# Set-up of a two-layer perceiver kernel: one load for all weights, X in quarters, row statistics moved into the first cross attention

## What is computed

```python
def _layernorm(x, axis=-1, eps=1e-05):
    m = jnp.mean(x, axis=axis, keepdims=True)
    v = jnp.var(x, axis=axis, keepdims=True)
    return (x - m) / jnp.sqrt(v + eps)

x = x + _L0_xattn_ref(ctx_1024, ctx_1024, _layernorm(x), Wk, Wv, bv, Wq, bq, Wo, bo)   # one head
x = x + _L0_attn_ref(_layernorm(x, axis=-1), ...)
...
```

## Time and profile before

| | |
|---|---|
| median of 3 runs | 1492.5 us (1491.97 to 1501.98) |
| profiled execution | 1493.61 us |
| its span, first to last instruction | 1491.8 us |
| mean granted clock of PE | 0.904 |
| busy: PE, DVE, ACT, POOL | 84%, 67%, 56%, 56% of the span |
| set-up pass | to about 28.8 us |
| first cross attention | about 28.8 to 136 us |

### The profile page before, as it was taken

One profiled execution on the slowest core, in us unless ns is written; L12 is line 12 of the kernel. 1 busy time (PEld: TensorE's weight loads), 2 busy tenths in 40 slices (PEclk: granted clock), 3 DMA queues, 4 the chain that ended last, 5 costly groups with the idle time before them and its releaser, 6 DMA issues. The chain is left out here.

```text
span 1491.8 us, 49249 instructions
## 1 busy us (share of the span) xinstructions
PE 1248.6 (84%) x15586; PEld 1084.6 (73%) x15587; DVE 1006.2 (67%) x3247; ACT 836.9 (56%) x2658; POOL 830.2 (56%) x1700
## 2 busy tenths in 40 slices
PE   3998698887489994999999999999969987369990
PEld 2777688776479993777777777777758877269990
DVE  4774378886446662788888788888759998523334
ACT  1664376664234442777777777777737776135550
POOL 2674035676646663566665666656434577736660
PEclk9997589997589996999999999999979999579995
DMA  7994651221122212322111111111000000122215
GB/s 236 328 361 145 228 157 53 69 69 44 57 64 64 66 54 65 97 65 81 35 38 50 35 53 35 41 47 32 16 16 3 17 29 27 59 56 71 67 59 176
DMA packets 93088, 121.84 MB, mean 82 GB/s; under 512 B 12402, under 2 KB 66931, under 8 KB 92947
## 3 DMA queue, kind: packets, MB, share of 16 engines
q1 hardware_dynamic: 74258, 82.70, 18.2%
q0 software_dynamic: 13312, 34.69, 6.5%
q10 hardware_dynamic: 5376, 2.63, 0.6%
HBM read 89.48 MB, written 30.49 MB: 80 GB/s over the span
## 5 line engine op out<-in xcount | busy, mean ns | idle before, releaser
L1611 ACT ACTIVATE p_prob<-six,p_nm 128x257 f32<-128x257 f32 x512 | 235.9, 474 | 121.5 <-DVE p_nm L1653 120.6
L1653 DVE TENSOR_REDUCE p_nm<-six 128x2 f32<-128x514 f32 x256 | 164.9, 685 | 36.4 <-PE six L1509 34.8
L1863 PE MATMUL bank<-sb_w,m_experts_aT 128*128 x1152 | 155.3, 278 | 2.7 <-ACT m_experts_aT L1892 2.2
L1842 POOL DMA_INDIRECT expert_outputs<-m_experts_y,m_experts_dest x144 | 142.3, 988 | 26.1 <-POOL m_experts_tiny L1841 15.8
L1879 PE MATMUL six<-m_experts_xT,m_experts_w 128*128 128x128 f32 x1152 | 156.0, 279 | 0.0
L791 POOL DMA_INDIRECT expert_inputs<-p_r_x,p_r_slot x128 | 126.2, 986 | 36.5 <-issue 35.6
L1863 PEld LDWEIGHTS bank<-sb_w,m_experts_aT 128*128 128x128 f32 x1152 | 141.3, 193 | 5.8 <-issue 5.6
L1879 PEld LDWEIGHTS six<-m_experts_xT,m_experts_w 128*128 128x128 f32 x1152 | 143.4, 196 | 0.5
L1530 PE MATMUL six<-sb_const,p_prob 128*128 128x128 f32 x1024 | 140.7, 281 | 0.0
L1390 POOL TENSOR_TENSOR p_score<-p_score,p_mx 128x512 f32<-128x512 f32 x64 | 67.1, 1049 | 124.6 <-DVE p_mx L1335 123.1
L1733 POOL TENSOR_TENSOR p_spread<-p_recip,sb_const 128x128 f32<-128x128 f32 x128 | 51.2, 400 | 150.2 <-DVE p_recip L1664 150.1
(11 more groups left out here) (293 smaller groups left out, 3504.5 us busy)
## 6 DMA issues: line engine op xcount, KB each, us to landing
ctxT_ring<-ctxT SPq DMA_DIRECT2D x32, 512.0 KB
ctxN_ring<-ctxN POOLq DMA_DIRECT2D x32, 512.0 KB, 5.5
p_ctxT<-ctxT SPq DMA_DIRECT2D x32, 512.0 KB, 3.6
m_experts_x<-expert_inputs SPq DMA_DIRECT2D x144, 64.5 KB
bd_scores<-p_rows SPq DMA_DIRECT2D x32, 256.0 KB, 2.9
p_bd<-bd_scores SPq DMA_DIRECT2D x32, 256.0 KB
sb_w<-w SPq DMA_DIRECT2D x32, 256.0 KB
p_y<-expert_outputs SPq DMA_DIRECT2D x32, 128.0 KB, 3.3
```

Of the source, the lines that this page charges most:

```text
L1611: last = nc.scalar.activation(prob[:, b, g, :], scores_ps[:, g, 0:CTX], ACT.Exp, bias=nm[:, b % 2, g:g + 1], accum_out=total[:, b % 2, g:g ...
L1653: nc.vector.tensor_reduce(nm[:, b % 2, g:g + 2], scores_ps[:, g:g + 2, 0:CTX], AX.X, ALU.max, negate=True).then_inc(s[most], 1)
L1842: nc.gpsimd.indirect_dma_start(m.ys_dram[:, :], bass.IndirectOffsetOnAxis(ap=dest[:, t.par:t.par + 1], axis=0), y[:, t.par, :], None).then ...
L1863: last = nc.tensor.matmul(ps[6 + t.two][:, 0:D], aT[:, t.two, f * P:(f + 1) * P], m.w2[:, DS(held[p] + f * D, D)], start=(f == 0), stop=(f ...
```

## The change

- The 18 weight matrices become one array of 128 rows of 9216 bytes, and SP loads it by one DMA. It and `const`, `cols`, `rows` are issued ahead of X.
- X is loaded in four quarters of 8 tiles. SP's order is now: quarter 0, context 0, quarter 1, context 1, context 2, quarter 2, context 3, quarter 3.
- In the set-up, DVE makes the statistics of quarter 0 alone, with each aggregation directly behind its own statistics, and POOL the factors and means of quarter 0 on 8 columns.
- In `cross_one_head`, DVE makes the statistics of two tiles in each of the steps 1 to 4, 9 to 12 and 17 to 20 (quarters 1, 2 and 3), between `z` and the maximum. POOL makes a quarter's factors and means in steps 5, 13 and 21, behind the step's context load. From tile 8 on, `z` waits for the factors of its quarter.

```diff
+        self.begun = 0
...
-    def dve_all(self, dve, x_in):
-
+    def dve_quarter(self, dve, q, tiles, bnst):
 
         m, nc = self.m, self.m.nc
-        for n in range(TILES + 1):
-            if n < TILES:
-                if n % HALF == 0:
-                    dve.wait_ge(x_in[n // HALF], 16)
-                if n >= 2:
-                    dve.wait_ge(self.kept, n - 1)
-                nc.vector.bn_stats(self.bnst[:, n % 2, :], m.X[:, n * D:(n + 1) * D]).then_inc(self.stats_done, 1)
-            if n >= 1:
-                dve.wait_ge(self.stats_done, n)
-                nc.vector.bn_aggr(m.mv_all[:, 2 * (n - 1):2 * n], self.bnst[:, (n - 1) % 2, :]).then_inc(self.kept, 1)
-
-    def pool_all(self, pool):
+        for n in tiles:
+            if n % QUARTER == 0:
+                dve.wait_ge(m.x_in[q], 16)
+            if self.begun >= 2:
+                dve.wait_ge(self.kept, self.begun - 1)
+            self.begun += 1
+            nc.vector.bn_stats(bnst[:, n % 2, :], m.X[:, n * D:(n + 1) * D]).then_inc(self.stats_done, 1)
+            dve.wait_ge(self.stats_done, self.begun)
+            nc.vector.bn_aggr(m.mv_all[:, 2 * n:2 * n + 2], bnst[:, n % 2, :]).then_inc(self.kept, 1)
+
+    def pool_quarter(self, pool, q, done):
+
         m, nc = self.m, self.m.nc
-        pool.wait_ge(self.kept, TILES)
-        mv = m.mv_all[:, :].rearrange("p (t k) -> p t k", k=2)
-        f = m.factor[:, :]
-        const = lambda k: m.const[:, k:k + 1].broadcast_to([P, TILES])
-        step = 0
-        for out, a, b in self.forms:
-            for dst, x, y, op in ((f, mv[:, :, 1], a, ALU.mult), (f, f, b, ALU.add), (out[:, :], f, C_POW, ALU.pow)):
-                if step:
-                    pool.wait_ge(self.pool_step, step)
-                nc.gpsimd.tensor_tensor(dst, x, const(y), op).then_inc(self.pool_step, 1)
-                step += 1
-        nc.gpsimd.tensor_tensor(m.MEAN[:, :], mv[:, :, 0], const(C_ONES), ALU.mult).then_inc(self.pool_step, 1)
+        pool.wait_ge(self.kept, QUARTER * (done + 1))
+        tiles = slice(q * QUARTER, (q + 1) * QUARTER)
+        mv = m.mv_all[:, 2 * q * QUARTER:2 * (q + 1) * QUARTER].rearrange("p (t k) -> p t k", k=2)
+        f = m.factor[:, tiles]
+        const = lambda k: m.const[:, k:k + 1].broadcast_to([P, QUARTER])
+        out, a, b = self.forms[0]
+        step = 4 * done
+        for dst, x, y, op in ((f, mv[:, :, 1], a, ALU.mult), (f, f, b, ALU.add), (out[:, tiles], f, C_POW, ALU.pow),
+                              (m.MEAN[:, tiles], mv[:, :, 0], C_ONES, ALU.mult)):
+            if step:
+                pool.wait_ge(self.pool_step, step)
+            nc.gpsimd.tensor_tensor(dst, x, const(y), op).then_inc(self.pool_step, 1)
+            step += 1
...
 RING, EARLY, ENDS = 4, 2, 8
+QUARTER = TILES // 4
...
-            for n in range(2):
-                sp.dma_start(m.X[:, n * 2048:(n + 1) * 2048].rearrange("p (t d) -> p t d", d=D),
-                             m.x_dram[n * 16:(n + 1) * 16].rearrange("t p d -> p t d")).then_inc(x_in[n], 16)
+            def quarter(q):
+                sp.dma_start(m.X[:, q * QUARTER * D:(q + 1) * QUARTER * D].rearrange("p (t d) -> p t d", d=D),
+                             m.x_dram[q * QUARTER:(q + 1) * QUARTER].rearrange("t p d -> p t d")).then_inc(m.x_in[q], 16)
+
+            def context(n):
+                sp.dma_start(m.ctxT[:, n], context_columns(m, n)).then_inc(m.columns_in[n], 16)
+                sp.dma_start(m.ends[:, n], context_ends(m, n)).then_inc(m.columns_in[n], 16)
+
             for dst, src in loads:
                 sp.dma_start(dst, src).then_inc(loaded, 16)
-            for n in range(RING):
-                sp.dma_start(m.ctxT[:, n], context_columns(m, n)).then_inc(m.columns_in[n], 16)
-                sp.dma_start(m.ends[:, n], context_ends(m, n)).then_inc(m.columns_in[n], 16)
+            quarter(0)
+            context(0)
+            quarter(1)
+            context(1)
+            for n in range(2, RING):
+                context(n)
+                quarter(n)
...
-            tail.dve_all(dve, x_in)
+            tail.dve_quarter(dve, 0, range(QUARTER), m.bnst)
...
-            tail.pool_all(pool)
+            tail.pool_quarter(pool, 0, 0)
...
+    m.in_use.extend(columns_in + rows_in + m.x_in)
...
+    given = Tail(m, "p1_given", [sinks(m, "z")])
...
+        given_stats = sb("given_stats", [P, 2, 6])
...
+                    if t.n >= QUARTER:
+                        dve.wait_ge(given.pool_step, 4 * (t.n // QUARTER))
                     normed(m, z[:, t.par, :], t, m.RZ).then_inc(s["z"], 1)
+                q, part = 1 + (n - 1) // QUARTER, (n - 1) % QUARTER
+                if n >= 1 and q < 4 and 2 * part < QUARTER:
+                    first = q * QUARTER + 2 * part
+                    given.dve_quarter(dve, q, range(first, first + 2), given_stats)
...
+                q = 1 + (n - 1) // QUARTER
+                if n % QUARTER == 1 + QUARTER // 2 and q < 4:
+                    given.pool_quarter(pool, q, q - 1)
...
-        m.w = {n: sb("w_" + n, [P, w]) for n, w in WEIGHTS.items()}
+        weights = sb("weights", [P, len(WEIGHTS) * P])
+        m.w = {n: weights[:, k * P:(k + 1) * P] for k, n in enumerate(WEIGHTS)}
         m.setup_loads = [(m.const[:, :], a["const"]), (m.cols[:, :], a["cols"]), (m.rows[:, :], a["rows"])]
-        m.setup_loads += [(m.w[n][:, :], a[n]) for n in WEIGHTS]
+        m.setup_loads += [(weights[:, :], a["weights"])]
...
+        m.x_in = [nc.alloc_semaphore(name=f"x_in_{n}") for n in range(4)]
...
+    a["weights"] = np.concatenate([a.pop(n) for n in WEIGHTS], 1)
```

More of the change, by code:

```diff
@@ L317, in setup_pass @@
     loaded = m.sem("weights_loaded")
-    x_in = [m.sem("x_in_a"), m.sem("x_in_b")]
     folded = m.sem("folded")
@@ L2065 @@
 COLS = ("bq0", "bv0", "bv_a", "bq_a", "bk_a", "u", "v", "gamma", "beta", "norm_w")
-WEIGHTS = {"Wq0": 128, "Wk0": 128, "Wv0": 128, "Wo0T": 128, "Wq_a": 128, "Wk_a": 128, "Wv_a": 128,
-           "Wpos": 128, "Wf": 128, "WqT_x": 128, "WkT_x": 128, "WvT_x": 128, "WoT_x": 128,
-           "w_q": 128, "w_k": 128, "w_v": 128, "w_o": 128, "ctx_last": 128}
+WEIGHTS = ("Wq0", "Wk0", "Wv0", "Wo0T", "Wq_a", "Wk_a", "Wv_a", "Wpos", "Wf", "WqT_x", "WkT_x", "WvT_x", "WoT_x",
+           "w_q", "w_k", "w_v", "w_o", "ctx_last")
 def lay_out(i):
```

1 line of the change is left out of this document (removed).

## The result

The changed kernel took 1487.4 us (median of 20 runs, 1483.1 to 1499.5), the kernel before 1494.1 us in the same comparison (20 runs, 1484.6 to 1502.0). The ratio is 0.9963, with a 95% interval of 0.9946 to 0.9979: by the ratio 5.5 us or 0.37% less (by the two medians 6.7 us), where I had forecast 9.5 us. The time is inside the range of 1478 to 1489 us, and it lies in the band of rival A too (1485.5 to 1490 us). The profiled execution of the changed kernel took 1488.0 us.

What follows compares the result with a forecast made beforehand. Two set-up chains, PE's weights and fold and the DVE/POOL row statistics, were taken as the bound to shorten. 10.2 us gained, less 0.5 and 0.2, is 9.5 us: 1483 us against the median, 1478 to 1489 us.

Steps and rivals of the forecast that it cites:

- rival A: Cross attention gives gain back through DVE's statistics pairs (2.3 to 6.7 us) or tiles blocked by POOL (3.4 us); chance 0.16.
- the slack of the context-row load: Cross attention, POOL's queue: load issued 9.7 us ahead of use, landing in 5.5 us, leaving 4.2 us of slack.
- the bursts: POOL making a quarter's factors and means in cross attention, 2.6 us each: cost 0.1 us per burst, 0.2 in all.
- The tile's own factor: Cross attention, queued behind POOL's quarter factors: 1.4 us of slack; DVE stands 0.8 us once, taken up by its gap.
- PE's chain decides: Set-up: PE's weights, fold and DVE's copies set the first normalised tile, 18.6 us, by half a microsecond or more.
- PE's start: Set-up: const and weights at 380 GB/s take 4.6 us plus 2.9 fixed, so PE starts at 8.4 us.
- The fold, the copies, eight columns of power: Set-up: fold unchanged at 6.29 us, first tile 3.91 us later; POOL's power on 8 columns takes 1.7 us.
- The pairs in DVE: Two tiles' statistics per cross-attention step: 0.84 us added, 0.09 us beyond the gap in full steps; 0.5 us in all.
- The order of the loads: SP issuing context tiles between and ahead of X's later quarters: everything lands in time, cost nothing.
- B: Set-up loads don't come earlier because large or many small rows jam SP's queue: 1489 to 1493 us; chance 0.06.
- C: PE's clock drops to 1.2 GHz, full steps up to 5.0 us: 1493 to 1515 us; chance 0.05.
- D: More gain than forecast: fold and first cross-attention steps at 2.4 GHz, 1475 to 1480 us; chance 0.13.

Runs made afterwards that it cites:

- load_ahead: Changed kernel with POOL issuing the context-row load first in its step, ahead of xb and the tile's factor: 1481.3 us, ratio 0.9932 against the kernel before.
- no_bursts: Changed kernel without POOL's factors for the last three quarters, DVE's statistics kept: single execution, no ratio; first to last maximum 88.24 us.
- loads_alone: Changed kernel's new loads, but all row statistics and factors in set-up: single execution, no ratio; first normalised tile 35.44 us, last maximum 127.63 us.
- the first two traces: Profiled executions of the changed kernel (ratio 0.9963) and of after_again; first to last maximum 91.86 and 95.24 us.
- after_again: Changed kernel run once more without any edit, for its trace: 1488.8 us (12 runs), ratio 0.9964 against the kernel before.
- statistics_alone: Changed kernel's moved statistics with the old separate weight loads and X ahead: single execution, no ratio; first normalised tile 28.69 us, last maximum 125.38 us.

## Why the forecast was right or wrong, step by step

By the last maximum the changed kernel is 5.2 us earlier, where the forecast had 9.5. Of the missing 4.3 us, 2.5 are the set-up's (7.7 us for 10.2) and 1.8 the cross attention's (2.5 us given back for 0.7). Of the set-up's 2.5, 1.9 are there already when PE starts (10.27 for 8.4 us), and 0.7 lie between DVE's first copy and the first tile (4.57 for 3.91 us).

**The first step that failed: the slack of the context-row load.** I wrote that it is "issued 3.3 steps or 9.7 us ahead of use and landing in 5.5 us: 4.2 us of slack", and so put the bursts at 0.2 us. I had matched the load at 81.43 us with the sum four behind the one at 79.39. By count of loads and sums it feeds the one three behind, at 88.23: 6.8 us, so 1.3 us of slack against the median landing, 0.2 against the slowest. A burst, whose power took 1.68 us as forecast (1.7), takes 1.95 us off that lead, and the landings at the third burst were slower than any before. The cost was 3.0 us in the first trace and 6.9 in the second, not 0.2. The tile's own factor, which I called the tight one, did make DVE wait, 0.51 us at the second burst and 1.16 us at the third, against my 0.8 us, and PE stood 0.83 us behind it (at 89.78 us, idle until DVE's copy to `pT`). But load_ahead has the same waits of DVE, 0.49 and 1.05 us, and hardly any loss: they weren't the cost.

**The second: what ends the set-up.** "PE's chain decides" was wrong, before and after. In the kernel before POOL's DRAIN ended at 28.0 us and DVE's at 27.2. DVE's copies ended 1.64 us and POOL's power 2.26 us ahead of the first tile, and 0.80 us is what the pause takes when nothing else is outstanding: both chains had 0.8 us or more to spare. What decided were POOL's two context-row loads, issued behind the weights at 18.88 us. They are issued 8.35 us earlier now and take 0.5 us longer to land (issue to last packet 8.7 us, then 9.2): 7.9 us, and the first tile moved by 7.70. The prediction counts these loads in the set-up's bytes, but nowhere as something that the pass ends with. Had DVE's chain decided in the changed kernel, the first tile would have come 0.80 us behind it, at 19.6 us.

**PE's start** was 10.27 us in this trace (9.02 to 10.27), outside my bounds of 7.9 to 9.8 in this one. The rate was mis-sized: 380 GB/s was taken between two rates of stretches with several loads under way, and a load left alone came in at 147 to 203. As loads were, the weights' arrival still mattered, because POOL waits for it to issue.

**The fold, the copies, eight columns of power** came as forecast: 6.28 us from PE's start to DVE's first copy (6.29), 1.67 us (1.7). DVE's eight tiles took 0.40 us each.

**The pairs in DVE**: forecast 0.5 us in all, measured nothing in no_bursts; the steps with pairs are 2.96 us, 0.01 to 0.02 over the even ones (3.00 the first). What I had given as 0.09 us a step beyond the gap didn't show as such.

**The order of the loads**: nothing late, as costed. Only together with all statistics in set-up (loads_alone) is it harmful.

**The rivals.** A (given back in the cross attention) is nearest to what came: 1487.4 us against its 1485.5 to 1490, but for the loss in POOL's queue, not for DVE's pairs or blocked tiles. Its mechanism of blocked tiles failed by a row: in the second burst, POOL's power runs from 59.69 to 61.37 us, and the timeline after has inside it

```profile
59.87 0.33 DVE L288 TENSOR_SCALAR p_z<-sb_X,sb_MEAN,sb_RN 128x128 f32<-128x128 f32 x1
60.12 0.34 DVE L288 TENSOR_SCALAR p_z<-sb_X,sb_MEAN,sb_RZ 128x128 f32<-128x128 f32 x1
```

at their usual length. The Trainium skill, "SBUF — State Buffer", section Who interferes with whom, by which a `tensor_scalar` in a two-port mode and a GpSimd instruction exclude each other, is not borne out by the power here; no row shows the mode of these two. Beside other work of POOL the same instruction was longer: 0.63 and 0.61 us at 65.86 and 66.41 us, where POOL issues a load and makes an `xb`. B did not happen. C's clock came in a way I had not drawn: not in the set-up, but behind PE's wait for a late load, in some executions. D's faster first steps came by luck of the trace: the third step is fast in eleven traces and slow in five, the same kernel being in both groups, and the 0.5 us that it gave between the first two traces are no effect of the change.

## What to carry to other kernels

Work added to a queue costs what stands behind it, and of these the loads first: count loads and users from the first to the last to get the lead, and compare the burst with lead minus the slowest landing, not with the median, knowing that the landings behind it may be slower still. A pass that ended in a barrier here waited for its last outstanding load from GpSimd's queue, so look at the DRAIN rows at its end; a load that only the next pass needs may be better issued there. And try a kernel's loads first in a step: it cost nothing here, gave nothing in the kernel before, and brought 2.4 us of the cross attention where bursts stood in the way.

## What the runs showed of the hardware that I had not expected

In ten of the traces the first tile behind the barrier followed the last packet of GpSimd's loads by 1.1 to 1.4 us, and in all it came 0.75 to 0.78 us behind the last engine's DRAIN. GpSimd's DRAIN took 2.81 us with its loads outstanding, 7.39 us with them issued late and 0.30 us without any. The barrier did not wait for SP's loads, which were still under way at 355 GB/s; SP's DRAIN took 0.12 us. One load of 128 rows of 9.2 KB ended at 147 to 203 GB/s with the DMA engines 0.35 to 0.51 busy, where several loads together reach over 400 GB/s. Where PE stood 3.35 us in the middle of steady work (after_again), the granted clock was 0.50 (1.2 GHz) for about 6 us behind it, from 95 to 101 us. It fell to 0.50 for about 3 us behind 1.91 us of standing too (statistics_alone, 103.5 to 106.5 us); after 1.39 us of standing in the changed kernel it stayed at 1.00. In the first steps of the cross attention sixteen matmuls took 1.08 us in some traces and 0.64 in others, with a granted clock of 1.00 shown for both.
